# A twelve-stage decoder on one core: sums of x columns ahead of key rotations, waits of query turns split by bank, query copies ahead of exponentials in the first four steps

## The chip, the cores and the metric

The kernel runs on one core of a Trainium2 chip, all in one launch. The metric is the device time of that launch in microseconds (us). TensorE is called PE here, VectorE DVE, ScalarE ACT, GpSimd POOL, SyncE (which only issues DMAs) SP. Each engine runs its own list of instructions in the order in which it is written; engines wait for one another on semaphores that only count up.

## The reference

A decoder of four layers over x of 8 batches x 128 tokens x 512 columns, in float32. Every layer is a self-attention, a cross-attention to a context `ctx` of the same shape, and a feed-forward part, each followed by a norm of the sum with x: 12 stages. The stages that the change touches are the end of stage 0 (an attention inside each token) and stages 1 and 4, the cross-attentions of the first two layers, with 32 query heads and 8 key/value heads of 128 columns each. Per batch:

```python
queries = (q @ Wq.T).reshape(B, Sq, 32, 128).transpose(0, 2, 1, 3)      # from x
keys    = (k @ Wk.T).reshape(B, Skv, 8, 128).transpose(0, 2, 1, 3)      # from ctx
values  = (v @ Wv.T).reshape(B, Skv, 8, 128).transpose(0, 2, 1, 3)
queries, keys = _rope(queries), _rope(keys)          # x * cos + rotated(x) * sin
scores = einsum('bhqd,bhkd->bhqk', queries, repeat(keys, 4)) * 128 ** -0.5   # + mask
ctx = softmax(scores) @ repeat(values, 4)
return ctx.reshape(B, Sq, 32 * 128) @ Wd.T           # added to x, then the norm
```

## The kernel before

`build` writes, stage by stage, one list of instructions for each engine; `cross` is the function of stages 1 and 4. A cross stage has 8 groups g (one key/value head and its 4 query heads each) and in a group 8 batches b: 64 units u = 8g + b. xT, the transposed x of 1024 columns, comes from the stage before: its norm turns x batch by batch on PE (`norm.turn`, L174) and ACT copies the result to xT (`norm.copy`, L179).

**Queries.** The 512 x 512 by 512 x 1024 product of a group is not done as 8 block products but as 7, on sums of blocks (Strassen's way): P1 to P7, each of 2 chunks, each chunk 2 passes of 512 columns in the trace (x4 records for a product). DVE makes the sums of blocks of xT once a stage (`sums_of_xT`, L942 to L946, for batches 4 to 6 and then for batch 7), POOL those of the query weights once a group (`wq_sums`, L1062 to L1068) and those of the output weights (`wo_sums`, L1042 to L1048). The work of a group is cut into six jobs q0 to q5, called turns: q0 to q2 for the first two heads (p = 0), q3 to q5 for the other two. In a turn PE writes one bank with P1, P6, P7, which add up there, and its neighbour bank with the other product (P2, then P5 and P3, then P4). ACT copies the neighbour bank into QT (`QT<-banks`, L841, signal `x_other_here`); DVE then adds the first bank to it (L916, signal `x_qadd`). Turns 0 and 3 make block C11, turns 1 and 4 make C22's part and C12, turns 2 and 5 make C21 and C22.

- Turns 0, 3: P2, P1. Turns 1, 4: P5, P6, P3. Turns 2, 5: P4, P7.
- In `queries` (L667 to L717) PE waits ahead of a turn's first product until the last block of the turn before has been added (`x_qadd`), for both banks.

**Rotation.** For each of 2 key halves and 8 query blocks of a group DVE makes the sine part in `turned` (L898, L899; two buffers, so that a rotation waits for the last but one on POOL) and POOL the rest (L1073 and L1075; keys only L1075). The cosine part of keys is DVE's (L907).

**A step** of the main loop (step s, L775 on PE): scores of unit s (L787); the first job of the next group; transposes of the probabilities of unit s-2 (L797); the product with V (L815); the other jobs; from step 4 on the output product of earlier units, two units at a time by 7 products (`products`, L761), and from unit 48 on one by one (`plain`, L745). ACT in a step: exponentials (L865), copy of the first job, copy of the turned probabilities (L847), copy of the mixed values (L876), scaling of the probabilities (L882), copies of the other jobs. DVE in a step: scale and mask (L1011), maximum (L1013), addition of the first job (L916), inverse of the sums (L1025), the step's rotations for the next group (`turn_some`, whose numbers for group 1 are (1,1,2,1,1,1,1,0)), additions of the other jobs.

Which job stands in which step is the table `plans` (L552): for group 1's jobs, done in steps 0 to 7, (2,1,2,1,1,0,1,0): q0 and q1 in step 0, q2 in step 1, q3 and q4 in step 2, q5 in step 3, values in steps 4 and 6. The opening (L764 to L774) has both key products of group 0, the turn of batch 7, the six turns of group 0 in the order q0, q3, q1, q4, q2, q5, the values, and the key products of group 1.

## Time and profile before

| | us |
|---|---|
| median of 3 runs | 2729.45 |
| lowest, highest | 2726.92, 2735.56 |
| the profiled execution | 2729.9 |
| its span in the profile | 2728.6 |

The profile is of one execution. All its times are us from the start of the span unless marked ns. A row of the timeline is a run of like instructions: start, duration, engine, line, operation, out<-in tiles and shapes, count, and in brackets how long the engine was idle before it and whose end it waited for. A float32 matmul of one chunk is 2 records. The end of the last matmul of a run is modelled, so that a row is 0.16 us longer than the time until PE can start the next. The granted clock is the share of 2.4 GHz that TensorE got.

| part of the span | from, to |
|---|---|
| opening of stage 1 on PE | 165.96 to 216.76 |
| its steps 0 to 3 | 216.76 to 256.06 |
| its steps from 4 on, to step 52 | 256.06 to 750 |
| opening of stage 4 on PE | 1116.85 to 1168.39 |
| its steps 0 to 3 | 1168.39 to 1207.69 |

### The profile page before, as it was taken

How to read it: one execution, taken by the hardware profiler on the slowest of the kernel's cores; microseconds unless marked ns; L12 is line 12 of the kernel's file. 1: busy time of each engine (PE TensorE's matmuls, PEld its weight loads, DVE VectorE, ACT ScalarE, POOL GpSimd, SP SyncE). 2: the span in 40 equal slices, each digit the busy share in tenths (PEclk: the TensorE clock that was granted, in tenths of full speed). 3: DMA queues.
4: the chain of work that ended last, by engine and by line, in shares of the span. 5: the costliest groups of instructions: out<-in, count | busy, mean ns of one | idle time of the engine just before them, and what ended most of it. 6: DMA issues, size and time to landing. Idle time of an engine off the chain costs nothing.

```text
span 2728.6 us, 40847 instructions
## 1 busy us (share of the span) xinstructions
PE 2595.4 (95%) x15544; PEld 1716.9 (63%) x15544; DVE 1576.0 (58%) x2953; ACT 1068.3 (39%) x3270; POOL 710.0 (26%) x695
## 2 busy tenths in 40 slices
PE   8989999999998898899999999989998889999998
PEld 7855676766565666456676675647774455666664
DVE  3476666676546456666666665464556653344455
ACT  0014444444462455244444444614444312333330
POOL 1036334444212000363334442122120220000002
PEclk9989999999999899999999999999999999999999
DMA  8631101111001100111011110010000010000000
GB/s 183 88 122 52 33 11 39 39 40 39 16 1 39 47 2 2 47 39 39 4 39 39 39 39 16 1 71 31 2 1 28 21 64 28 15 27 1 12 1 31
DMA packets 53826, 94.91 MB, mean 35 GB/s; under 512 B 29408, under 2 KB 38560, under 8 KB 47488
## 3 DMA queue, kind: packets, MB, share of 16 engines
q1 hardware_dynamic: 53632, 92.30, 11.5%
q8 instruction: 125, 2.05, 0.3%
q14 instruction: 69, 0.57, 0.1%
HBM read 83.89 MB, written 8.39 MB: 34 GB/s over the span
## 4 chain that ended last, share of the span: by engine, by line
PE 87%; DVE 7%; ACT 3%; issue 1%; DMA 1%; POOL 0%; DVEq 0%; SPq 0%; POOLq 0%; ACTq 0%
PE banks L683 14%; PE banks L761 11%; PE banks L664 4%; PE banks L745 4%; PE banks L815 4%; PE banks L787 4%; PE banks L651 4%; PE banks L1922 3%; PE banks L303 3%; PE banks L1411 3%; PE banks L1974 3%; PE banks L2212 2%; PE banks L1951 2%; PE banks L2244 2%; PE banks L1927 2%; PE banks L2277 2%
## 5 line engine op out<-in xcount | busy, mean ns | idle before, releaser
L161 POOL TENSOR_TENSOR norm_spread<-norm_mv,const 128x1 f32<-128x1 f32 x96 | 20.8, 217 | 1173.0 <-DVE norm_mv L157 1173.0
L865 ACT ACTIVATE E_x<-S_x,sm_x 128x128 f32<-128x128 f32 x512 | 199.3, 390 | 283.6 <-DVE sm_x L1013 282.2
L1073 POOL TENSOR_TENSOR QT<-QT,const 128x512 f32<-128x512 f32 x128 | 170.2, 1330 | 503.4 <-DVE turned L899 503.4
L683 PE MATMUL banks<-xT,weights 128*128 128x512 f32 x512 | 238.9, 601 | 10.3 <-DVE QT L916 10.3
L977 DVE TENSOR_TENSOR x<-banks,x 128x256 f32<-128x256 f32 (+1 forms) x288 | 147.2, 511 | 125.4 <-PE banks L761 121.4
L761 PE MATMUL banks<-weights,OT 128*128 128x256 f32 x768 | 189.4, 379 | 0.0
L916 DVE TENSOR_TENSOR QT<-banks,QT 128x512 f32<-128x512 f32 x128 | 85.4, 688 | 160.6 <-ACT QT L841 148.5
L683 PEld LDWEIGHTS banks<-xT,weights 128*128 128x128 f32 x512 | 95.4, 192 | 121.2 <-issue 106.7
L1075 POOL TENSOR_TENSOR QT<-QT,turned 128x512 f32<-128x512 f32 x128 | 166.5, 1301 | 10.0
L876 ACT ACTIVATE OT<-banks 128x512 f32<-128x512 f32 x128 | 76.5, 597 | 229.3 <-PE banks L815 229.3
L761 PEld LDWEIGHTS banks<-weights,OT 128*128 128x128 f32 x768 | 141.8, 190 | 38.3 <-DVE x L977 11.7
L882 ACT ACTIVATE E_x<-E_x,sm_x 128x128 f32<-128x128 f32 x512 | 162.1, 390 | 5.3 <-DVE sm_x L1025 5.3
L2340 ACT ACTIVATE E_s<-banks,top_s 128x128 f32<-128x128 f32 x512 | 139.3, 383 | 62.1 <-DVE top_s L2437 62.1
L683 PE MATMUL banks<-weights 128*128 128x512 f32 x320 | 155.7, 602 | 2.2 <-DVE QT L916 2.1
L787 PEld LDWEIGHTS banks<-KT,QT 128*128 128x128 f32 x1024 | 133.9, 191 | 18.3 <-issue 13.4
L761 PE MATMUL banks<-weights 128*128 128x256 f32 x576 | 144.2, 386 | 0.0
L815 PE MATMUL banks<-PT,V 128*128 128x512 f32 x256 | 131.1, 593 | 4.3 <-ACT PT L847 4.3
L787 PE MATMUL banks<-KT,QT 128*128 128x128 f32 x1024 | 134.9, 275 | 0.0
L761 PEld LDWEIGHTS banks<-weights 128*128 128x128 f32 x576 | 102.6, 190 | 43.4 <-DVE x L977 27.6
L841 ACT ACTIVATE QT<-banks 128x512 f32<-128x512 f32 x128 | 75.2, 588 | 125.3 <-PE banks L683 124.9
L2333 ACT ACTIVATE PT_s<-banks 128x512 f32<-128x512 f32 x128 | 69.8, 596 | 137.3 <-PE banks L2277 137.3
L899 DVE TENSOR_TENSOR turned<-QT,const 64x512 f32<-64x512 f32 x128 | 120.8, 944 | 1.8
(311 smaller groups left out, 5219.8 us busy)
## 6 DMA issues: line engine op xcount, KB each, us to landing
weights<-in_L_xwq SPq DMA_DIRECT2D x16, 1024.0 KB, 4.9
weights<-in_L_xwo SPq DMA_DIRECT2D x16, 1024.0 KB, 4.9
weights<-in_L_xwk SPq DMA_DIRECT2D x16, 256.0 KB, 5.1
weights<-in_L_xwv SPq DMA_DIRECT2D x16, 256.0 KB, 2.6
weights<-in_L_ffn_W_base SPq DMA_DIRECT2D x3, 1024.0 KB, 4.8
weights<-in_L_xwq SPq DMA_DIRECT2D x4, 768.0 KB, 5.0
weights<-in_L_xwo SPq DMA_DIRECT2D x4, 768.0 KB, 5.7
xT<-in_xT SPq DMA_DIRECT2D x4, 512.0 KB, 9.6
```

The source lines that it names most:

```text
L651: mm = PE.matmul(psum[keys_bank(g, i)][:, :], views["wk"][:, k, :], ctxT[:, k, half_of(i)], start=k == 0, stop=k == KC - 1)
L683: mm = PE.matmul(to, left[:, k, head], moving, start=name in ("P1", "P2", "P4", "P5") and k == 0, stop=k == 1, skip_group_check=name in (" ...
L761: mm = PE.matmul(to, left[:, k, :], right[:, k, :], start=first and k == 0, stop=k == 1, skip_group_check=name in ("P6", "P7", "P3"))
L787: mm = PE.matmul(psum[2 + u % 2][:, rows_of(h)], QT[g % 2][:, h, rows_of(b)], KT[g % 2][:, rows_of(b)], start=True, stop=True)
L815: PE.matmul(psum[5][:, :], V[g % 2][:, b, :], PT[u % 2][:, :, :], start=True, stop=True).then_inc(*x_mix.one())
L865: ins = AC.activation(e[:, j, :], s[:, j, :], ACT.Exp, bias=sm[:, 0, j:j + 1], scale=1.0, accum_out=sm[:, 1, j:j + 1])
L882: ins = AC.activation(e[:, j, :], e[:, j, :], ACT.Copy, scale=sm[:, 2, j:j + 1])
L899: return DV.tensor_tensor(t[lo, :, :], four(source[hi, :]), spread(sin128[hi, :], 4), ALU.mult)
L977: DV.tensor_tensor(to, source, to, ALU.add).then_inc(*x_sum.one())
L1073: PO.tensor_tensor(four(to), four(to), spread(cos128, 4), ALU.mult).then_inc(*pool_step.one())
L1075: PO.tensor_tensor(four(to), four(to), turned[j % 2][:, :, :], ALU.add).then_inc(*x_roped.one())
L2340: ins = AC.activation(E[s % 2][:, 4 * half + j, :], scores_of(half)[:, j // 2, j % 2, :], ACT.Exp, bias=top[s % 2][:, 4 * half + j:4 * hal ...
```

## The change

1. **Opening, PE.** In stage 1 batch 6 of x is turned after the first key product of stage 1 and no longer at the end of stage 0; so the first key product stands ahead of it.
2. **Opening, DVE.** The sums of xT of batch 7 stand ahead of the key rotations. The two key rotations stand behind the additions of q0 and q3, and the first query rotation behind the second of them.
3. **Waits by bank.** In `queries` PE waits ahead of a turn's first product (neighbour bank) for ACT's copy of that bank alone, and for DVE's addition only ahead of the first product into the other bank. This holds for all groups.
4. **Steps 0 to 3.** The table of jobs becomes (1,1,2,2,1,0,1,0): q0, q1, q2 and q3, q4 and q5. On PE the second job stands ahead of the product with V. ACT copies the first job's blocks ahead of the exponentials, and scales ahead of the second job and of the copy of the mixed values. The numbers of `turn_some` stay.
5. **First plain product** (unit 48). PE waits for one addition less, that into columns 0 to 255 of x from the neighbour bank.

```diff
@@ heads: pe_heads
-                    for b in range(4, 7):
+                    for b in range(4, 6):
                         norm.turn(b)
@@ cross
-                plans = [(2, 1, 2, 1, 1, 0, 1, 0)] + [(2, 2, 1, 2, 1, 1, 1, 0)] * (G8 - 2)
+                plans = [(1, 1, 2, 2, 1, 0, 1, 0)] + [(2, 2, 1, 2, 1, 1, 1, 0)] * (G8 - 2)
+                def no_outs(step):
+                    return step < 4
@@ pe_cross: queries
-                        if turn:
-                            PE.wait_ge(*x_qadd(8 * g + place_of(g, p, ADDED[turn - 1][-1]) + 1))
-                        elif g and n:
-                            PE.wait_ge(*x_qadd(8 * g + 4))
                         if n == 1:
                             PE.wait_ge(*xwq_sums(g + 1))
                             if g == 0:
                                 PE.wait_ge(*xT_sums(2))
+                        if turn:
+                            PE.wait_ge(*x_other_here(8 * g + place_of(g, p, OTHER[turn - 1][-1], OTHER) + 1))
+                            sums_added = x_qadd(8 * g + place_of(g, p, ADDED[turn - 1][-1]) + 1)
+                        elif g and n:
+                            PE.wait_ge(*x_other_here(8 * g + 4))
+                            sums_added = x_qadd(8 * g + 4)
+                        else:
+                            sums_added = None
                         if turn == 0:
                             product("P2").then_inc(*x_other.one())
+                            if sums_added:
+                                PE.wait_ge(*sums_added)
                             product("P1").then_inc(*x_query.one())
                         elif turn == 1:
                             product("P5").then_inc(*x_other.one())
+                            PE.wait_ge(*sums_added)
                             product("P6")
...
                             product("P4").then_inc(*x_other.one())
+                            PE.wait_ge(*sums_added)
                             product("P7").then_inc(*x_query.one())
@@ pe_cross: plain
-                            PE.wait_ge(*x_sum(NA * pairs + u - 2 * pairs))
+                            PE.wait_ge(*x_sum(NA * pairs + u - 2 * pairs - (u == 2 * pairs)))
@@ pe_cross: opening and steps
-                    for kind, i in opening[:2]:
-                        job(0, kind, i)
+                    job(0, "k", 0)
+                    if stage == 1:
+                        before.turn(B - 2)
+                    job(0, "k", 1)
                     before.turn(B - 1)
...
                         plain(step, 0)
+                        if no_outs(step):
+                            for j in jobs_at(step, 1):
+                                job(*j)
...
                             PE.matmul(psum[5][:, :], V[g % 2][:, b, :], PT[u % 2][:, :, :], start=True, stop=True).then_inc(*x_mix.one())
-                        for j in jobs_at(step, 1):
-                            job(*j)
+                        if not no_outs(step):
+                            for j in jobs_at(step, 1):
+                                job(*j)
@@ act_cross (exps, mixed_copy, scale hold what stood in the loop before)
                     for step in range(units + 3):
+                        if no_outs(step):
+                            for j in jobs_at(step, 0):
+                                drain(*j)
+                            exps(step)
+                            if step >= 2:
+                                turned_copy(step - 2)
+                            scale(step)
+                            for j in jobs_at(step, 1):
+                                drain(*j)
+                            if step >= 2:
+                                mixed_copy(step - 2)
+                            continue
@@ dve_cross: opening
                     sums_of_xT(4, B - 1)
-                    for kind, i in opening[:2]:
-                        drain(0, kind, i)
                     sums_of_xT(B - 1, B)
                     done = 0
                     for n, (kind, i) in enumerate(opening[2:]):
                         drain(0, kind, i)
-                        while done < (1, 2, 3, 4, 5, 8)[n]:
+                        if n < 2:
+                            rope_keys(0, n)
+                        while done < (0, 2, 3, 4, 5, 8)[n]:
                             turn_queries(0, done)
                             done += 1
```

What stands in a row on PE at the end of stage 0 and the start of stage 1 (L336 is stage 0's last product, L174 the turns of x, L651 the key products, L683 the query products), before:

```order
L336 MATMUL banks<-const,o 64x64 x32
L174 MATMUL banks<-const,x 128x128 x12
L651 MATMUL banks<-ctxT,weights 128x512 x8
L174 MATMUL banks<-const,x 128x128 x4
L683 MATMUL banks<-xT,weights 128x512 x10
```

and now (L655 and L687 are the former L651 and L683):

```order
L336 MATMUL banks<-const,o 64x64 x32
L174 MATMUL banks<-const,x 128x128 x8
L655 MATMUL banks<-ctxT,weights 128x512 x4
L174 MATMUL banks<-const,x 128x128 x4
L655 MATMUL banks<-ctxT,weights 128x512 x4
L174 MATMUL banks<-const,x 128x128 x4
L687 MATMUL banks<-xT,weights 128x512 x10
```

The first key product, four records of the list, moved up over the turn of batch 6.

ACT from step 0 of stage 1 on (L865 exponentials, L841 a copy of a query block, L882 the scaling), before:

```order
L865 ACTIVATE E0_x1,sm0_x1<-S0_x1,sm0_x1 128x128 x4
L841 ACTIVATE QT1_1<-banks 128x512
L882 ACTIVATE E0_x1<-E0_x1,sm0_x1 128x128 x4
L841 ACTIVATE QT1_1<-banks 128x512 x2
L865 ACTIVATE E1_x1,sm1_x1<-S1_x1,sm1_x1 128x128 x4
L841 ACTIVATE QT1_1<-banks 128x512
L882 ACTIVATE E1_x1<-E1_x1,sm1_x1 128x128 x4
```

and now (L880, L861, L893 in their place):

```order
L861 ACTIVATE QT1_1<-banks 128x512
L880 ACTIVATE E0_x1,sm0_x1<-S0_x1,sm0_x1 128x128 x4
L893 ACTIVATE E0_x1<-E0_x1,sm0_x1 128x128 x4
L861 ACTIVATE QT1_1<-banks 128x512 x2
L880 ACTIVATE E1_x1,sm1_x1<-S1_x1,sm1_x1 128x128 x4
L893 ACTIVATE E1_x1<-E1_x1,sm1_x1 128x128 x4
L861 ACTIVATE QT1_1<-banks 128x512
```

The copies of the first job moved up over the exponentials, and with the new table the two copies of q1 stand in step 1.

DVE from step 2 of stage 1 on (L1011 mask, L1013 maximum, L916 an addition of a query block, L1025 inverse, L898 and L899 a rotation), before:

```order
L1011 SCALAR_TENSOR_TENSOR S0_x1<-banks,const 128x512
L1013 TENSOR_REDUCE sm2_x1<-S0_x1 128x4
L916 TENSOR_TENSOR QT1_1<-banks,QT1_1 128x512
L1025 RECIPROCAL sm2_x1<-sm2_x1 128x4
L898 TENSOR_TENSOR turned0_1<-QT1_1,const 64x512
L899 TENSOR_TENSOR turned0_1<-QT1_1,const 64x512
L898 TENSOR_TENSOR turned1_1<-QT1_1,const 64x512
L899 TENSOR_TENSOR turned1_1<-QT1_1,const 64x512
L916 TENSOR_TENSOR QT1_1<-banks,QT1_1 128x512
```

and now (L1050, L1052, L955, L1064, L937 and L938):

```order
L1050 SCALAR_TENSOR_TENSOR S0_x1<-banks,const 128x512
L1052 TENSOR_REDUCE sm2_x1<-S0_x1 128x4
L955 TENSOR_TENSOR QT1_1<-banks,QT1_1 128x512 x2
L1064 RECIPROCAL sm2_x1<-sm2_x1 128x4
L937 TENSOR_TENSOR turned0_1<-QT1_1,const 64x512
L938 TENSOR_TENSOR turned0_1<-QT1_1,const 64x512
L937 TENSOR_TENSOR turned1_1<-QT1_1,const 64x512
L938 TENSOR_TENSOR turned1_1<-QT1_1,const 64x512
L955 TENSOR_TENSOR QT1_1<-banks,QT1_1 128x512
```

The additions ahead of the two rotations are now the two of q2; the one behind them, which was q4's, is now q3's.

## Rows read from the trace of the kernel before

**Rows 1.** The page: busy time, chain by engine, two groups on GpSimd.

```profile
PE 2595.4 (95%) x15544; PEld 1716.9 (63%) x15544; DVE 1576.0 (58%) x2953; ACT 1068.3 (39%) x3270; POOL 710.0 (26%) x695
...
PE 87%; DVE 7%; ACT 3%; issue 1%; DMA 1%; POOL 0%; DVEq 0%; SPq 0%; POOLq 0%; ACTq 0%
...
L1073 POOL TENSOR_TENSOR QT<-QT,const 128x512 f32<-128x512 f32 x128 | 170.2, 1330 | 503.4 <-DVE turned L899 503.4
...
L1075 POOL TENSOR_TENSOR QT<-QT,turned 128x512 f32<-128x512 f32 x128 | 166.5, 1301 | 10.0
```

**Rows 2.** Timeline of PE, first cross opening (start, us, line, tiles, count, idle before).

```profile
163.99 1.97 PE L174 MATMUL banks<-const,x 128*128 128x128 f32 x8
168.17 0.66 PE L174 MATMUL banks<-const,x 128*128 128x128 f32 x4 [2.21 <-DVE x L167]
168.66 8.73 PE L651 MATMUL banks<-ctxT,weights 128*128 128x512 f32 x16
...
177.67 7.03 PE L683 MATMUL banks<-xT,weights 128*128 128x512 f32 x16
185.47 1.98 PE L683 MATMUL banks<-xT,weights 128*128 128x512 f32 x4 [0.77 <-DVE QT L916]
...
202.74 7.31 PE L664 MATMUL banks<-weights,ctxT 128*128 128x128 f32 x64
```

**Rows 3.** Windows: busy us by engine, granted clock (PEclk), DMA share, GB/s.

```profile
163.30:166.70 3.40, 2.66 (x22) 2.14 (x18) 2.14 (x5) 1.20 (x2) 0.00 (x0) 0.62 0.01 2
...
169.30:172.71 3.41, 3.41 (x5) 1.35 (x4) 3.41 (x3) 0.16 (x1) 3.24 (x3) 0.50 0.72 193
216.76:256.06 39.30, 33.49 (x101) 16.54 (x100) 23.12 (x32) 16.27 (x55) 23.61 (x18) 0.96 0.05 13
223.91:227.32 3.41, 3.41 (x5) 1.35 (x4) 1.41 (x2) 1.42 (x4) 2.00 (x3) 0.50 0.02 5
256.06:640.00 383.94, 383.90 (x1739) 265.95 (x1737) 259.59 (x452) 180.18 (x592) 158.70 (x120) 1.00 0.09 31
```

**Rows 4.** Timeline of DVE in the same opening.

```profile
169.96 1.61 DVE L942 TENSOR_TENSOR weights<-xT 128x384 f32<-128x384 f32 x1
...
177.40 0.68 DVE L898 TENSOR_TENSOR turned<-banks,const 64x512 f32<-64x512 f32 x1
...
181.74 1.38 DVE L944 TENSOR_TENSOR xT<-xT 128x128 f32<-128x128 f32 x1
...
184.74 0.68 DVE L916 TENSOR_TENSOR QT<-banks,QT 128x512 f32<-128x512 f32 x1
```

**Rows 5.** Timeline of PE, the waits of the first steps.

```profile
223.38 3.30 PE L683 MATMUL banks<-xT,weights 128*128 128x512 f32 x4 [2.14 <-DVE QT L916]
...
231.91 1.12 PE L683 MATMUL banks<-weights 128*128 128x512 f32 x2 [0.52 <-DVE QT L916]
...
242.58 1.13 PE L815 MATMUL banks<-PT,V 128*128 128x512 f32 x2 [1.45 <-ACT PT L847]
```

**Rows 6.** Timeline of ACT: a query copy behind the exponentials.

```profile
221.96 0.58 ACT L841 ACTIVATE QT<-banks 128x512 f32<-128x512 f32 x1
```

**Rows 7.** Timeline of DVE: half a rotation beside a busy GpSimd.

```profile
247.62 1.66 DVE L899 TENSOR_TENSOR turned<-QT,const 64x512 f32<-64x512 f32 x1
```

**Rows 8.** Timeline of POOL: sums of query weights, sums of output weights.

```profile
216.33 1.27 POOL L1062 TENSOR_TENSOR weights<-weights 128x512 f32<-128x512 f32 x1
...
241.10 1.27 POOL L1042 TENSOR_TENSOR weights<-weights 128x512 f32<-128x512 f32 x1
```

**Rows 9.** Timeline of PE, opening of the second cross stage.

```profile
1135.59 3.50 PE L683 MATMUL banks<-xT,weights 128*128 128x512 f32 x4 [4.30 <-DVE QT L916]
...
1154.38 7.31 PE L664 MATMUL banks<-weights,ctxT 128*128 128x128 f32 x64
```

**Rows 10.** Timeline of PE: the first plain product.

```profile
737.29 3.67 PE L745 MATMUL banks<-weights,OT 128*128 128x512 f32 x8 [0.97 <-DVE x L977]
```

**Rows 11.** Timeline of DVE: the last addition ahead of it.

```profile
736.73 0.41 DVE L977 TENSOR_TENSOR x<-banks,x 128x256 f32<-128x256 f32 x1
```

47 lines of the change are left out of this document (25 added, 22 removed).

## The prediction, worked out before the change ran

> **What bounds the kernel now.** I read the page first: PE is busy for 95% of the span and holds 87% of the chain that ended last [rows 1]. An edit therefore pays only where PE stands idle, or runs at the lower clock, inside the two cross stages. The windows say where that is: from 256.06 to 640.00 PE is busy for 383.90 of 383.94 us [rows 3]. The waits split by bank apply to every group, but in the groups of this stretch there is no wait to take away: worth 0 there. What is left are two openings, two times four first steps, and the first plain product.
>
> In the opening of stage 1 [rows 2] PE is idle for 2.21 us before the turn of batch 6. The key products behind it take 8.73 us, where the 16 like passes from 177.67 on take 7.03, because the granted clock was 0.50 from 169.30 to 172.71 [rows 3]. Then comes a wait of 0.77 us at 185.47, for DVE. In steps 0 to 3 PE is busy for 33.49 of 39.30 us [rows 3], so 5.81 are idle (the longest 2.14, 0.52 and 1.45 [rows 5]), and again the clock was 0.50, from 223.91 to 227.32 [rows 3]. 3.41 us at half clock are 1.7 us of work lost, of which 1.6 can be had back where PE waits a little anyway. Each restart also hides 0.16 us of modelled end. The work in these steps is 56 query passes (7.03/16 less the tail, 0.43 each, 24.0), 4 passes with V (1.7), 4 scores (3.6) and 2 transposes (0.9): 30.2. So 9.1 us a stage is all that the steps can give.
>
> **The openings.** *Stage 1, PE.* The last turn of stage 0 ends at 163.99 + 1.97 = 165.96 [rows 2]. Now the first key product (8 passes, 3.44) starts there, ends at 169.4, and the turn of batch 6 follows, whose norm was done at 168.1. The context and the weights are there: the DMA share from 163.30 to 166.70 is 0.01 [rows 3]. No idle 2.21 us, so I also expect no low clock behind it: second key product to 173.3, turn 7, q0 and q3 from 173.7 to 180.6 (before 177.67 to 184.54): **3.9 gained**. *DVE.* The sums of xT need batch 6's copy, now at 170.7 instead of 169.5, so they start 0.8 later than at 169.96 [rows 4], while POOL is busy less long beside them; they end at about 177.8 (before 177.40). The small sums took from 181.54 to 184.74, with one subtraction of 1.38 us beside POOL [rows 4]; they now follow at once, with POOL idle: 2.1 us, end 180.0. PE wants them at 180.6. The 0.77 + 0.16 is gone: **0.9**. *The price* is that the key rotations (2.1 each, 177.40 to 181.54 [rows 4]) and all that POOL does come later: the first query rotation reaches POOL at 187.7, not 186.9. POOL needs 1.33 + 1.30 = 2.63 us for a block [rows 1], DVE two halves of 0.7, or 1.66 beside POOL [rows 7]. Walking through the eight blocks with the two `turned` buffers I get POOL's last end at about 212.6, before 216.33 [rows 8]; PE reaches its scores at 216.76 - 4.9 = 211.9. The scores need six blocks, ready at 206.5. But the sums of the next query weights, 5.3 us from 216.33 on [rows 8], now end at 217.9, and PE wants them for q1 at 217.1: a new wait of 0.9 in step 0, the first place where the price is paid. *Stage 4* has the turn of batch 6 earlier already, so only DVE's part counts: the wait of 4.30 us before 1135.59, and the slow passes behind it (3.50 us for 4 records, 1.88 elsewhere) [rows 9]; PE would go on at 1131.3. q5 then ends at 1148.3 instead of 1154.38 [rows 9]: **6.1**. DVE is 0.8 us further ahead here, and the wait for the weight sums is about 0. Sum of the openings 3.9 + 0.9 + 6.1 = **10.9**.
>
> **Steps 0 to 3.** t counts from the start of scores 0. Step 0 of before: ACT copies q0's block at 221.96, behind the exponentials, although P2 was done at 219.4 [rows 6], DVE adds, and PE starts q1 at 223.38 [rows 5]. Now that copy is ahead, q1 moves into step 1 behind the scores, and the sum is added at t 5.3: the 2.14 and the low clock behind it go. In stage 1 q1 runs from 6.1 (weight sums) to 11.3. q2 follows scores 2 at 12.1: ACT's copy of C12 (12.0) and DVE's addition (12.75) are there for P4 and P7. DVE then does rotation 1, mask and maximum and both additions of q2 by 17.9; PE's P1 of q3 wants them at 17.8: wait 0.2. Then the expensive place. q3 is now a second job, so on DVE its addition stands behind `turn_some` of step 2, with two rotations, just when POOL is in the sums of the output weights (four operations from 241.10 on [rows 8], some 6 us). Half a rotation takes 1.66 us there [rows 7], so the two end 6.6 us after 18.45, q3's addition at 25.75, and PE, which has done P5 of q4 at 23.2, waits for P6: **2.6 us of new idle**. q5 then waits 0.4 for the copy of C12, which stands ahead of the exponentials. Scores 4 start at 34.5 in stage 1, 33.7 in stage 4, where before they started at 39.3: **4.8 and 5.6**. The move of the second job ahead of the product with V costs nothing: that product waits for ACT's copy of the turned probabilities (1.45 us, [rows 5]), which q3 now covers. From step 4 on DVE's mask comes 1.0 us behind the scores as before, and POOL is ahead of where it was.
>
> Which value for the 2.6? Its ends are 0, if DVE's halves take 0.7, and 3.5, if POOL's output sums and the next blocks hold both rotations throughout; I take 2.6, from the row that is the same operation at the same place. GPSIMD Engine Reference of the Trainium skill, section 1 (Specifications), says that GpSimd shares its SBUF interfaces with VectorE, in contention with instructions that have two SBUF inputs; by that rule a table which puts a rotation ahead of an addition under POOL's sums speaks against the change, and without it the forecast would be 5 us lower.
>
> **After an idle of 2.6 us** the clock may fall once more. It fell behind 2.21, 2.14 and 4.30 and not behind 0.77 or 1.45. A low stretch costs 1.6. I take it in one of the two stages: **-1.6**, ends 0 and -3.2.
>
> **The plain product.** PE waits 0.97 us at 737.29 [rows 10] for an addition that DVE ends at 737.14 [rows 11]. The remaining wait was met before, so each stage gains 0.97 + 0.16: **2.3**.
>
> **Sum.** 10.9 + 4.8 + 5.6 - 1.6 + 2.3 = 22.0. The profiled execution took 2729.9 (span 2728.6 and 1.3 around it), the median is 2729.45, which is 0.45 lower. 2729.9 - 22.0 = **2708**.
>
> **Rivals.**
> *The steps give nothing.* Each wait for an addition turns into one for POOL's weight sums, a copy or the exponentials behind the copy. Only the openings and the plain product stay: 13.2, 2717. For it: my walk already has four new waits in a stage. Against it: only one is long. 12%.
> *No wait is left in the steps.* 10.9 + 18.2 + 2.3 = 31.4 gained would be 2698.5; with some small waits 2701. It needs rotations at 0.7 us beside a busy POOL. 10%.
> *Low clock behind every short wait.* In the rows 0.52 and 0.77 left the clock high. TensorE: Matmul & The Clock Gate of the Trainium skill, on its second failure mode (psum-queue depth-cycling), says that frequent micro-idles between groups of matmuls make the clock oscillate. In this kernel that would be a low stretch behind each of my seven new waits: 23.6 - 7 x 1.6 = 12.4 gained, 2717.5. 5%.
> *The sums don't decide.* If in the opening PE, freed from the sums, waits as long for q0's addition at P6, about 5 us per stage come back: 2718. Against it: the addition is DVE's next operation behind the sums. 6%.
> *Slower.* The later key rotations push POOL's chain. Scores 0 need six query blocks, of which POOL starts the first at 187.7 and PE wants the last at 211.9: 4.0 us a block. If DVE's half pair beside POOL (3.3) and POOL's pair (2.6) came one after the other, a block would take 5.9, the scores would wait 11.4 a stage: 2708 + 22.8 + 1.6 = 2732. It decides from 4.0 us a block. Against it: two `turned` buffers let them overlap, and the mean of POOL's block is 2.63 [rows 1]. Even more than 5.9 is needed for slower by over 0.3%. 5%.
>
> **How the numbers follow.** Forecast 62%, the rivals 12, 10, 5, 6 and 5. The range takes the forecast's own bounds (2703 to 2713) and reaches to the rivals on both sides: 2701 to 2718, leaving out the slower case and the outer edges, under 2 in 10. About 0.3% (8 us, so 2721 and 2738) is what a measurement of this kernel can tell from no change. Faster 0.87 (all but the slower case and the upper edges of three rivals), same 0.10, slower 0.03.
>
> **What would show it.** Right: no idle ahead of the first key product and none at q1 in the openings; no granted clock of 0.50 between the first key product and scores 0; a PE wait of 2 to 3 us for a DVE addition in the middle of q4 of step 3; scores 4 of stage 1 some 9.7 us earlier than 256.06, those of stage 4 some 11.7 us earlier in their own stage; no wait ahead of the plain product. Wrong: PE waits at q1 of step 0 or 1 for POOL's weight sums by more than 2 us, or at scores 0 for a rotation, or any wait in steps 4 to 8 that was not there before.

## The result and the profile after

The changed kernel takes 2711.98 us (median of 4 runs, 2711.70 to 2717.03), the kernel before on the same chip 2730.48 (4 runs); the ratio is 0.9935 with a 95% interval of 0.9915 to 0.9955. The profiled execution took 2711.99 us, its span is 2710.7, 17.9 less than 2728.6. The forecast was 2708, 22.0 less.

The page of the changed kernel (busy time; chain that ended last) answers to [rows 1]:

```profile
PE 2587.2 (95%) x15544; PEld 1715.8 (63%) x15544; DVE 1582.3 (58%) x2953; ACT 1067.7 (39%) x3270; POOL 715.1 (26%) x695
...
PE 85%; DVE 8%; ACT 3%; issue 2%; POOL 1%; DMA 1%; DVEq 0%; SPq 0%; POOLq 0%; ACTq 0%
```

PE is still busy for 95% of a shorter span; GpSimd has come into the chain with 1%, and DVE has 8% of it. Where GpSimd stands in the chain shows in the timeline of PE in stage 1 (start, us, line, tiles, count, idle before and its releaser), against [rows 2, 5]:

```profile
165.28 3.70 PE L655 MATMUL banks<-ctxT,weights 128*128 128x512 f32 x8 [0.78 <-DVE x L422]
...
173.13 8.75 PE L687 MATMUL banks<-xT,weights 128*128 128x512 f32 x20
...
211.18 1.05 PE L803 MATMUL banks<-KT,QT 128*128 128x128 f32 x8
...
219.72 3.58 PE L687 MATMUL banks<-xT,weights 128*128 128x512 f32 x4 [3.16 <-POOL weights L1107]
...
240.81 1.98 PE L687 MATMUL banks<-weights 128*128 128x512 f32 x4 [2.13 <-DVE QT L955]
...
245.20 1.13 PE L687 MATMUL banks<-weights 128*128 128x512 f32 x2 [0.25 <-ACT QT L861]
...
249.59 1.05 PE L803 MATMUL banks<-KT,QT 128*128 128x128 f32 x8
```

The opening did what was foreseen. The first key product starts at 165.28 instead of behind the turn of batch 6. The idle of 0.78 ahead of it, for a DVE addition, was not foreseen, but it costs nothing here: the turns in front took 1.09 us, where before they took 1.97, partly at the lower clock, so the product starts 5.7 us behind the start of stage 0's last product, where the forecast had 5.8. And the 0.77 ahead of q1 in the opening is gone, since q0, q3 and the first of q1 are one row of 20 records; scores 0 start at 211.18. The wait of 2.14 us for q0's addition is gone too. In its place, at 219.72, PE waits 3.16 us for GpSimd's weight sums. The wait of P6 in q4 that was foreseen is there (2.13 at 240.81), and so is the small one for the copy of C12 (0.25).

Stage 4, against [rows 9]: no wait in the opening (it was 4.30 us), and the same two long ones in the steps.

```profile
1117.34 8.75 PE L687 MATMUL banks<-xT,weights 128*128 128x512 f32 x20
...
1163.48 1.98 PE L687 MATMUL banks<-xT,weights 128*128 128x512 f32 x4 [2.71 <-POOL weights L1107]
...
1182.80 1.98 PE L687 MATMUL banks<-weights 128*128 128x512 f32 x4 [1.96 <-DVE QT L955]
```

Windows of the changed kernel (busy us of PE, PEld, DVE, ACT, POOL; granted clock; DMA share; GB/s): steps 0 to 3 of stage 1, the low clock in them, 32 later steps of that stage, steps 0 to 3 of stage 4. They answer to [rows 3]:

```profile
211.18:249.59 38.41, 32.86 (x101) 16.39 (x100) 26.39 (x37) 17.25 (x59) 27.77 (x21) 0.96 0.03 7
219.55:222.97 3.42, 3.25 (x4) 1.51 (x5) 2.14 (x3) 1.33 (x5) 2.57 (x3) 0.50 0.00 0
359.00:680.27 321.27, 321.27 (x1442) 221.18 (x1441) 219.03 (x377) 149.11 (x489) 137.72 (x104) 1.00 0.10 34
1155.39:1191.59 36.20, 31.27 (x102) 15.74 (x101) 25.77 (x37) 17.24 (x59) 27.62 (x21) 1.00 0.03 7
```

The low clock of the opening and that of before from 223.91 on are gone; one stands behind the new 3.16 us wait, none behind the 2.71 of stage 4 or the two of 2.13 and 1.96.

And the first plain product, against [rows 10]:

```profile
728.78 3.60 PE L759 MATMUL banks<-weights,OT 128*128 128x512 f32 x8
```

It follows the products ahead of it with no idle.

The start of PE's rows gives the account by stretch. All are differences of the profiled executions, in us; "left as it is" is the part of the span that runs the same code in both.

| stretch | before | after | difference | forecast |
|---|---|---|---|---|
| stage 0's last product to scores 0 | 56.64 | 51.64 | -5.0 | -4.9 |
| steps 0 to 3, stage 1 | 39.30 | 38.41 | -0.9 | -4.8 |
| steps 4 to 47, stage 1 | 431.59 | 430.68 | -0.9 | 0 |
| steps 48 to 62, stage 1 | 126.89 | 125.68 | -1.2 | -1.1 |
| first key product to scores 0, stage 4 | 51.54 | 45.46 | -6.1 | -6.1 |
| steps 0 to 3, stage 4 | 39.30 | 36.20 | -3.1 | -5.6 |
| steps 4 to 47, stage 4 | 431.39 | 430.76 | -0.6 | 0 |
| steps 48 to 62, stage 4 | 126.93 | 125.71 | -1.2 | -1.1 |
| left as it is | 1425.0 | 1426.1 | +1.1 | 0 |
| low clock charged ahead of time | | | | +1.6 |
| sum | 2728.6 | 2710.7 | -17.9 | -22.0 |

Two things did not come as forecast. The first four steps gave 4.0 us instead of 10.4, or instead of 8.8 when the low clock that the forecast charged apart is counted with them (one such stretch is in the 38.41). And the later steps gave 1.5 us that nobody had forecast.

### The profile page after: what moved, and what is told of

Its sections match the earlier page's. It is cut to its first block, busy times and chain, and to the rows that moved or that the text cites. A ratio compares the mean times of both kernels' runs of the same rounds, so it can differ in the third digit from the quotient of the medians.

```text
span 2710.7 us, 40847 instructions
## 1 busy us (share of the span) xinstructions
PE 2587.2 (95%) x15544; PEld 1715.8 (63%) x15544; DVE 1582.3 (58%) x2953; ACT 1067.7 (39%) x3270; POOL 715.1 (26%) x695
## 4 chain that ended last, share of the span: by engine, by line
PE 85%; DVE 8%; ACT 3%; issue 2%; POOL 1%; DMA 1%; DVEq 0%; SPq 0%; POOLq 0%; ACTq 0%
PE banks L687 13%; PE banks L775 11%; PE banks L759 4%; PE banks L834 4%; PE banks L803 4%; PE banks L668 4%; PE banks L655 3%; PE banks L1961 3%; PE banks L1450 3%; PE banks L303 3%; PE banks L2013 3%; PE banks L2251 2%; PE banks L2283 2%; PE banks L1990 2%; PE banks L1966 2%; PE banks L2316 2%
## 5 line engine op out<-in xcount | busy, mean ns | idle before, releaser
L880 ACT ACTIVATE E_x<-S_x,sm_x 128x128 f32<-128x128 f32 x512 | 199.2, 390 | 262.0 <-DVE sm_x L1052 260.5
L687 PE MATMUL banks<-xT,weights 128*128 128x512 f32 x512 | 236.7, 596 | 5.9 <-POOL weights L1107 5.9
L687 PEld LDWEIGHTS banks<-xT,weights 128*128 128x128 f32 x512 | 95.0, 191 | 113.6 <-issue 105.8
L775 PEld LDWEIGHTS banks<-weights,OT 128*128 128x128 f32 x768 | 141.8, 190 | 38.3 <-DVE x L1016 11.7
L893 ACT ACTIVATE E_x<-E_x,sm_x 128x128 f32<-128x128 f32 x512 | 162.1, 390 | 1.0 <-DVE sm_x L1064 1.0
L955 DVE TENSOR_TENSOR QT<-banks,QT 128x512 f32<-128x512 f32 x128 | 85.3, 687 | 129.6 <-ACT QT L861 127.7
L687 PE MATMUL banks<-weights 128*128 128x512 f32 x320 | 153.2, 594 | 4.6 <-DVE QT L955 4.1
L803 PEld LDWEIGHTS banks<-KT,QT 128*128 128x128 f32 x1024 | 133.9, 191 | 18.3 <-issue 13.2
L861 ACT ACTIVATE QT<-banks 128x512 f32<-128x512 f32 x128 | 75.3, 588 | 142.7 <-PE banks L687 142.3
L938 DVE TENSOR_TENSOR turned<-QT,const 64x512 f32<-64x512 f32 x128 | 130.4, 1018 | 1.8
```

The lines of the kernel that those rows point to most:

```text
L687: mm = PE.matmul(to, left[:, k, head], moving, start=name in ("P1", "P2", "P4", "P5") and k == 0, stop=k == 1, skip_group_check=name in (" ...
L775: mm = PE.matmul(to, left[:, k, :], right[:, k, :], start=first and k == 0, stop=k == 1, skip_group_check=name in ("P6", "P7", "P3"))
L803: mm = PE.matmul(psum[2 + u % 2][:, rows_of(h)], QT[g % 2][:, h, rows_of(b)], KT[g % 2][:, rows_of(b)], start=True, stop=True)
L880: ins = AC.activation(e[:, j, :], s[:, j, :], ACT.Exp, bias=sm[:, 0, j:j + 1], scale=1.0, accum_out=sm[:, 1, j:j + 1])
L893: ins = AC.activation(e[:, j, :], e[:, j, :], ACT.Copy, scale=sm[:, 2, j:j + 1])
L938: return DV.tensor_tensor(t[lo, :, :], four(source[hi, :]), spread(sin128[hi, :], 4), ALU.mult)
```

## Experiments

**The question.** The openings gave 11.1 us, the steps behind them 6.4 too little (4.8, if the low clock that the forecast charged apart is counted with them). *Theory:* the edit of DVE's opening puts the key rotations later, the chain of rotations on DVE and GpSimd does not become shorter with PE's way, and GpSimd's sums of the next query weights, which stand behind that chain, become the last thing that q1 waits for. Then the openings' gain is partly given back. *Rival:* the new order of the steps gives little by itself, whatever the opening. First each part alone, and the wait itself.

### The steps without the opening edits

```diff
@@ the changed kernel
-                    for b in range(4, 6):
+                    for b in range(4, 7):
                         norm.turn(b)
-                    job(0, "k", 0)
-                    if stage == 1:
-                        before.turn(B - 2)
-                    job(0, "k", 1)
+                    for kind, i in opening[:2]:
+                        job(0, kind, i)
...
                     sums_of_xT(4, B - 1)
+                    for kind, i in opening[:2]:
+                        drain(0, kind, i)
                     sums_of_xT(B - 1, B)
...
-                            PE.wait_ge(*x_sum(NA * pairs + u - 2 * pairs - (u == 2 * pairs)))
+                            PE.wait_ge(*x_sum(NA * pairs + u - 2 * pairs))
```

> The changed kernel with both opening edits and the plain product as in the kernel before: the new table of jobs, ACT's and PE's new order in steps 0 to 3 and the waits by bank stay. Theory (price of the later key rotations): GpSimd is not pushed back here, its sums of the next query weights end some 4.9 us behind the start of scores 0 as before, and q1 wants them at 5.2, so PE has no wait on GpSimd in step 0 or 1. Steps 0 to 3 then take 33 to 34 us in each cross stage (39.3 before, 38.4 and 36.2 after), and the kernel some 11 to 13 us less than before, about 2718. Rival (the new order of the steps itself gives little): 36 us or more per stage with a wait of 2 us or more of another name, and at most 7 us gained.

The windows of its steps 0 to 3 in stages 1 and 4:

```profile
215.11:248.50 33.39, 31.00 (x101) 15.69 (x100) 23.89 (x33) 17.24 (x59) 24.85 (x19) 1.00 0.03 9
1165.20:1198.43 33.23, 31.00 (x101) 15.67 (x100) 23.75 (x33) 17.24 (x59) 24.70 (x19) 1.00 0.03 8
```

33.4 and 33.2 us, at full clock throughout: 5.9 and 6.1 less than before. The only wait of more than 0.3 us in each is the one of q4, here stage 1's:

```profile
239.72 1.99 PE L687 MATMUL banks<-weights 128*128 128x512 f32 x4 [2.14 <-DVE QT L953]
```

So the new steps, which here include the waits by bank, are worth 6 us a stage, as long as GpSimd is not late. The rival falls. (The waits by bank alone, two sections on, take 3.4 of these 5.9 us in stage 1; the new order by itself was not run.) The kernel as a whole took 2723.81 us (ratio 0.9968, 0.9955 to 0.9982), less of a gain than the 11 to 13 expected: its cross stages are 13.2 us shorter, but the code that is the same in all kernels took 6.3 us more in its profiled execution (see the last section).

### The opening edits alone

```diff
@@ the kernel before
-                    for b in range(4, 7):
+                    for b in range(4, 6):
                         norm.turn(b)
-                    for kind, i in opening[:2]:
-                        job(0, kind, i)
+                    job(0, "k", 0)
+                    if stage == 1:
+                        before.turn(B - 2)
+                    job(0, "k", 1)
...
                     sums_of_xT(4, B - 1)
-                    for kind, i in opening[:2]:
-                        drain(0, kind, i)
                     sums_of_xT(B - 1, B)
                     done = 0
                     for n, (kind, i) in enumerate(opening[2:]):
                         drain(0, kind, i)
-                        while done < (1, 2, 3, 4, 5, 8)[n]:
+                        if n < 2:
+                            rope_keys(0, n)
+                        while done < (0, 2, 3, 4, 5, 8)[n]:
```

> The kernel before with the two opening edits alone. Both theories: openings 5.0 and 6.1 us shorter. Theory: GpSimd's weight sums then end about 8.5 us behind the start of scores 0, and q1, which before waited until 6.6 for its addition, now waits until 8.5 for them: steps 0 to 3 take about 41 us instead of 39.3, and the kernel gains 7 to 8 us (about 2722). Rival: the steps stay at 39.3 and the gain is 11 us.

Windows of its steps 0 to 3, PE's row at q1, and GpSimd's last weight sum:

```profile
212.61:254.13 41.52, 33.49 (x101) 16.58 (x100) 25.32 (x35) 16.25 (x55) 26.23 (x20) 0.96 0.06 13
1164.64:1206.14 41.50, 33.49 (x102) 16.52 (x100) 25.15 (x35) 16.25 (x55) 26.05 (x20) 0.96 0.05 13
```

```profile
221.46 3.68 PE L683 MATMUL banks<-xT,weights 128*128 128x512 f32 x4 [4.36 <-DVE QT L918]
```

```profile
218.93 1.26 POOL L1070 TENSOR_TENSOR weights<-weights 128x512 f32<-128x512 f32 x1
```

The openings are 4.2 and 5.7 us shorter. The steps take 41.5 us in both stages, 2.2 more than before, close to the 41 of the theory. But the last thing q1 waited for was not the weight sums, ready at 220.2; it was q0's addition at 221.4. Both hang on the same chain: DVE can rotate the second key half of group 1 only when GpSimd has given the `turned` buffer of the last block back, and mask, maximum, exponentials, copy and addition come behind that. The stretch with the same code as before cost 9.6 us more here, and the kernel took 2732.59 us (ratio 1.0000, 0.9989 to 1.0011): instead of the 7 to 8 us that were expected, this edit on its own could not be told from no change, though PE's way through the cross stages had become 5.5 us shorter in the profile.

### The waits by bank alone

```diff
@@ the kernel before
                     def queries(g, n):
-                        if turn:
-                            PE.wait_ge(*x_qadd(8 * g + place_of(g, p, ADDED[turn - 1][-1]) + 1))
-                        elif g and n:
-                            PE.wait_ge(*x_qadd(8 * g + 4))
+                        if turn:
+                            PE.wait_ge(*x_other_here(8 * g + place_of(g, p, OTHER[turn - 1][-1], OTHER) + 1))
+                            sums_added = x_qadd(8 * g + place_of(g, p, ADDED[turn - 1][-1]) + 1)
+                        elif g and n:
+                            PE.wait_ge(*x_other_here(8 * g + 4))
+                            sums_added = x_qadd(8 * g + 4)
...
```

> The kernel before with the waits by bank alone. In the steps of all later groups PE had no idle to give. In steps 0 to 3 P5 of q1 can start before q0's addition, but ACT's copy stands behind the exponentials and the addition follows it by 0.1 us, so the 2.14 us wait shrinks by 0.8 at most, and the other waits of 0.5 go: 1 to 2.5 us per stage. In the openings the wait for the x sums is the last one and stays. 2 to 5 us in all, about 2726. If more than 8 us are gained, the waits by bank are the change's main part.

```profile
216.12:252.05 35.93, 31.09 (x102) 15.87 (x101) 22.61 (x32) 16.20 (x55) 23.61 (x18) 1.00 0.06 15
361.35:682.63 321.28, 321.28 (x1442) 221.32 (x1441) 218.99 (x377) 149.01 (x489) 137.71 (x104) 1.00 0.10 34
1167.52:1205.07 37.55, 32.72 (x102) 16.50 (x101) 22.46 (x32) 16.24 (x55) 23.45 (x18) 0.95 0.06 13
```

Steps 0 to 3 take 35.9 us in stage 1 (-3.4) and 37.6 in stage 4 (-1.8, with a low clock in it that costs 1.7). That is more than I expected; the wait at q1 shrank from 2.14 to 1.43 and took its low clock along. The middle row is the surprise: steps 16 to 47 take 321.28 us, where the kernel before took 322.36. PE counts as busy for 322.32 of the one and all of the other, at the same clock, so what went are idles too short to be shown as waits, 0.27 us a group. The changed kernel has the same 321.27. Against this, steps 4 to 7 take 0.4 us longer, with a new wait of 0.35 for an addition to x. In all its cross stages are 6.5 us shorter, and the kernel took 2727.49 us (ratio 0.9988, 0.9977 to 0.9999), 2.2 less than the kernel before, where 2 to 5 were expected.

### The wait for the weight sums cut in three

```diff
@@ the changed kernel, queries
                         if n == 1:
-                            PE.wait_ge(*xwq_sums(g + 1))
+                            PE.wait_ge(*xwq_first(g + 1))
...
                             product("P5").then_inc(*x_other.one())
                             PE.wait_ge(*sums_added)
+                            if n == 1:
+                                PE.wait_ge(*xwq_third(g + 1))
                             product("P6")
+                            if n == 1:
+                                PE.wait_ge(*xwq_sums(g + 1))
@@ wq_sums
-                        PO.tensor_tensor(a21, a21, a22, ALU.add).then_inc(*pool_step.one())
-                        PO.wait_ge(*pool_step.all())
-                        PO.tensor_tensor(QS[:, 0], a21, a11, ALU.subtract).then_inc(*pool_step.one())
-                        PO.wait_ge(*pool_step.all())
+                        PO.tensor_tensor(a21, a21, a22, ALU.add).then_inc(*xwq_first.one())
+                        PO.wait_ge(*xwq_first(g + 1))
+                        PO.tensor_tensor(QS[:, 0], a21, a11, ALU.subtract).then_inc(*xwq_third.one())
+                        PO.wait_ge(*xwq_third(g + 1))
```

> The changed kernel with PE's wait for the weight sums cut into three: P5 waits for the second of GpSimd's four operations, P6 for the third, P3 for the fourth. Theory: P5 of q1 starts 2.7 us earlier, where GpSimd's second operation ends; the waits of 3.16 and 2.71 us shrink to about 0.6 and 0.1 and the low clock behind the first goes: 5 to 7 us less than the changed kernel, about 2705.5. Rival (something else is as late, such as the addition of q0 or the copy): under 2 us gained.

```profile
217.60 1.99 PE L688 MATMUL banks<-xT,weights 128*128 128x512 f32 x4 [0.46 <-POOL weights L1108]
...
222.31 1.96 PE L688 MATMUL banks<-xT,weights 128*128 128x512 f32 x4 [1.02 <-ACT QT L866]
...
238.97 1.98 PE L688 MATMUL banks<-weights 128*128 128x512 f32 x4 [2.13 <-DVE QT L960]
```

The 3.16 us wait became 0.46, and no low clock followed. But 1.02 us came back three products later, for ACT's copy of C22: on ACT that copy stands behind exponentials and scaling, and P5 now ends before they do. Steps 0 to 3 take 36.0 us in stage 1 (38.4) and 37.1 in stage 4, where this time a low clock stands behind the wait of q4 (35.4 without it). The kernel took 2709.34 us (ratio 0.9925, 0.9910 to 0.9940): the expected 5 to 7 us were about 3 in the steps, since a part of the wait was owed to the next in line.

### GpSimd's cosine products of the opening left out

```diff
@@ the changed kernel, pool_cross
-                            rope(NR * g + 2 + m, query(g, *rotated(g)[m]), True)
+                            rope(NR * g + 2 + m, query(g, *rotated(g)[m]), g > 0)
```

> The changed kernel with GpSimd's cosine product of the eight query blocks of group 0 left out (so the rotation of these blocks is incomplete): 8 operations of 1.3 us less on GpSimd in each opening, nothing changed on PE, ACT and DVE. Theory (the chain of rotations on GpSimd and DVE in the opening, 3.6 us a block, makes the weight sums late): the chain ends 5 us or more earlier, the waits of 3.16 and 2.71 us at q1 and the low clock go, and steps 0 to 3 take 33.2 to 33.6 us in both stages, as without the opening edits; about 2704. Rival (the weights' load or DVE's own list, not GpSimd, is late): a wait of over 1 us at q1 stays.

```profile
210.75:245.83 35.08, 32.70 (x101) 16.27 (x100) 22.90 (x33) 17.25 (x59) 20.54 (x16) 0.95 0.03 8
235.93:239.35 3.42, 3.42 (x6) 1.36 (x5) 0.69 (x1) 0.00 (x0) 3.34 (x3) 0.50 0.00 0
1150.39:1183.62 33.23, 31.01 (x102) 15.67 (x100) 22.75 (x33) 17.25 (x59) 20.38 (x16) 1.00 0.02 8
```

With GpSimd's chain some 8 operations shorter and PE's, ACT's and DVE's lists untouched, both waits at q1 are gone; the waits left in the steps are 2.13 (1.97) and 0.25. Stage 4's steps take 33.2 us, stage 1's 35.1 with a low clock from 235.93 on, 33.4 without. These are the times of the kernel without opening edits. So it is the chain of rotations with GpSimd in it, not the load of the weights nor DVE's list by itself, that takes 5.0 and 3.0 us of the openings' 11.1 back. The edit does not part GpSimd's own time from what it does to DVE: with the products gone, four of DVE's eight second halves in the opening of stage 1 fell from 1.66 to 0.69 us too. The two runs took 2704.00 and 2708.71 us.

### DVE's opening undone in the changed kernel

```diff
@@ the changed kernel
                     sums_of_xT(4, B - 1)
+                    for kind, i in opening[:2]:
+                        drain(0, kind, i)
                     sums_of_xT(B - 1, B)
                     done = 0
                     for n, (kind, i) in enumerate(opening[2:]):
                         drain(0, kind, i)
-                        if n < 2:
-                            rope_keys(0, n)
-                        while done < (0, 2, 3, 4, 5, 8)[n]:
+                        while done < (1, 2, 3, 4, 5, 8)[n]:
```

> The changed kernel with DVE's opening as before: key rotations ahead of the sums of batch 7 and of the query blocks. Theory: the wait for the x sums comes back (3.7 to 4.2 us in stage 1, 3.7 in stage 4, each with a low clock), but GpSimd has started its rotations earlier against PE, so the waits for the weight sums go: openings 4 and 6 us longer, steps 5 and 3 us shorter than in the changed kernel. Net +2 to +4 us, about 2715. Rival (DVE's new opening brings its full 7 to 10 us): 2719 or more.

PE's row at q1 of the opening, and the windows of steps 0 to 3 ("issue" says that the profile shows no releaser; DVE's last sum of x ends at 184.17, 0.1 us ahead of the row):

```profile
184.27 3.09 PE L687 MATMUL banks<-xT,weights 128*128 128x512 f32 x4 [4.18 <-issue]
```

```profile
217.22:252.30 35.08, 32.70 (x101) 16.25 (x100) 23.88 (x33) 17.25 (x59) 24.85 (x19) 0.95 0.03 8
1159.81:1194.74 34.93, 32.70 (x102) 16.26 (x101) 23.75 (x33) 17.25 (x59) 24.70 (x19) 0.95 0.03 8
```

The exchange is as the theory has it: a wait of 4.18 us for the x sums comes back in the opening (3.75 in stage 4), the wait for the weight sums goes, and the steps take 35.1 and 34.9 us, each with a low clock that costs 1.7; without it 33.4 and 33.2. The size is between the two expectations: openings 6.1 and 5.7 us longer, steps 3.3 and 1.3 shorter, cross stages 7.3 us longer than in the changed kernel, 5.6 if the low clocks in the steps of both are left out. The kernel took 2717.73 us (ratio 0.9952, 0.9937 to 0.9967). So DVE's new opening is worth 6 to 7 of the 11.8 us that its own stretches show.

Set side by side, the profiles of stage 1 also say what in the opening makes the sums late. All times count from the start of stage 0's last product:

| | first query rotation on GpSimd | weight sums ready | scores 0 | sums behind scores 0 |
|---|---|---|---|---|
| the kernel before | 26.8 | 61.5 | 56.6 | 4.9 |
| the changed kernel | 27.3 | 60.1 | 51.6 | 8.5 |
| DVE's opening undone | 26.8 | 62.7 | 57.8 | 4.9 |
| without cosine products | 27.3 | 52.0 | 51.7 | 0.3 |

The chain starts within 0.5 us of the same place in all four. The later key rotations hardly move it; the sums are even ready 1.4 us earlier than before. They are late only against PE, which is at scores 0 5.0 us earlier.

### A rotation out of step 2

The other wait, 2.1 us ahead of P6 of q4, is the one that the prediction had from DVE's row of rotations.

```diff
@@ the changed kernel
-                shares = [(1, 1, 2, 1, 1, 1, 1, 0)] + [(0, 1, 1, 2, 1, 1, 1, 1)] * (G8 - 2)
+                shares = [(1, 1, 1, 1, 2, 1, 1, 0)] + [(0, 1, 1, 2, 1, 1, 1, 1)] * (G8 - 2)
```

> The changed kernel with one of the two rotations of step 2 moved to step 4 (numbers 1,1,1,1,2,1,1,0). Theory (q3's addition is late because two rotations of 1.66 us halves stand ahead of it on DVE): the waits of 2.13 and 1.96 us ahead of P6 of q4 go, 4 us less in all, about 2708; steps 4 to 8 stay at 29.1 us. Rival (the rotations are wanted where they were): steps 4 to 8 take 1 us or more longer.

```profile
259.29 1.13 PE L775 MATMUL banks<-weights 128*128 128x256 f32 x4 [1.41 <-DVE x L1016]
...
269.33 1.13 PE L775 MATMUL banks<-weights,OT 128*128 128x256 f32 x4 [0.56 <-DVE weights L999]
```

The wait went in both stages (steps 0 to 3: 36.0 and 33.9 us, 2.4 and 2.3 less). But steps 4 to 7 take 30.9 us instead of 29.1: the rotation now stands ahead of an addition to x, for which PE waits 1.41, and ahead of the sums of mixed values (0.56). 1.8 of 2.3 us were handed to the next step; the rival was right on this half. 2710.05 us (0.9922, 0.9905 to 0.9938).

Both small edits together:

> Both small edits together: PE's wait for the weight sums cut in three, and a rotation moved from step 2 to step 4. Theory: they add up, 36.0 us of the steps in stage 1 become 33.8 and 35.4 (at full clock) in stage 4 become 33.3: 2.5 us from the one and 4 us from the other, about 2705.

They add up in the steps: 33.5 and 33.1 us, at full clock, behind them 30.9 as with the rotation alone. 2706.97 us (0.9914, 0.9896 to 0.9932).

### Where the rotation may go

Two more places for that rotation, with the wait cut in three, and the changed kernel again on the same chip:

```diff
-                shares = [(1, 1, 1, 1, 2, 1, 1, 0)] + [(0, 1, 1, 2, 1, 1, 1, 1)] * (G8 - 2)
+                shares = [(1, 1, 1, 1, 1, 2, 1, 0)] + [(0, 1, 1, 2, 1, 1, 1, 1)] * (G8 - 2)
@@ or
+                shares = [(1, 1, 1, 1, 1, 1, 1, 1)] + [(0, 1, 1, 2, 1, 1, 1, 1)] * (G8 - 2)
```

> As the kernel with the wait cut in three and one rotation moved, but the rotation is moved to step 5 (numbers 1,1,1,1,1,2,1,0), where DVE has no sums of mixed values ahead of it and no query block to add. Theory (in step 4 the second rotation stood ahead of an addition to x, PE waited 1.4 and 0.6 us there): steps 4 to 8 fall from 30.9 to 29.1 to 29.5 us, steps 0 to 3 stay at 33.1 to 33.5; 3 us less over both stages. Rival (any second rotation in steps 4 to 7 costs the same): 30.5 us or more.

```profile
266.21 1.10 PE L780 MATMUL banks<-weights,OT 128*128 128x256 f32 x4 [1.17 <-DVE x L1021]
269.21 2.07 PE L780 MATMUL banks<-weights,OT 128*128 128x256 f32 x4 [1.90 <-DVE weights L1004]
```

Step 5 is the worst of the places tried: waits of 1.17 and 1.90 us, in stage 1 a low clock with the second, and 33.2 and 31.9 us for steps 4 to 7. The rival was right. My reason was true and not enough: the sums of mixed values stand in steps 4 and 6, not in 5, but step 5 has additions to x, and the sums of step 6 come close behind its rotations. DVE's list shows it:

```profile
265.63 0.42 DVE L1021 TENSOR_TENSOR x<-banks,x 128x256 f32<-128x256 f32 x1
...
267.29 0.41 DVE L1001 TENSOR_TENSOR weights<-banks,OT 128x256 f32<-128x256 f32 x1
```

The rotations end at 265.61 and the addition for which PE waits stands right behind them; the sums of mixed values follow from 267.29. The kernel took 2718.55 us (0.9951, 0.9938 to 0.9964).

> The same with the last rotation of group 1 in step 7 (numbers 1,1,1,1,1,1,1,1), so that no step has two. Theory: steps 4 to 8 at 29.0 to 29.3 us, steps 8 to 16 at 80.3 as long as GpSimd has the last block by step 12. Within 1 us of the kernel with two rotations in step 5.

Windows of steps 0 to 3 and 4 to 7, stage 1 and stage 4:

```profile
211.62:245.22 33.60, 31.56 (x101) 15.77 (x100) 22.97 (x35) 17.26 (x59) 24.51 (x19) 1.00 0.03 9
245.22:273.84 28.62, 28.62 (x178) 24.30 (x176) 21.05 (x40) 16.25 (x56) 14.73 (x12) 1.00 0.14 47
1150.72:1183.91 33.19, 31.57 (x102) 15.77 (x101) 22.56 (x35) 17.25 (x59) 24.38 (x19) 1.00 0.03 8
1183.91:1212.52 28.61, 28.61 (x178) 24.27 (x177) 21.04 (x40) 16.25 (x56) 14.70 (x12) 1.00 0.15 47
```

One rotation in each step leaves PE busy for all of steps 4 to 7 (28.62 of 28.62 us) and 33.6 and 33.2 us for steps 0 to 3. Its two cross stages take 1275.8 us, 8.7 less than those of the changed kernel (1284.5), and its time is below that of the kernel before and of the changed kernel: 2708.02 us (0.9913, 0.9900 to 0.9927), where the changed kernel on the same chip had 2716.72. Against the kernel with the second rotation in step 4 (0.9914, on another chip) its cross stages are 4.4 us shorter, but the total does not show it.

> The changed kernel once more, on the same chip as the two above, for a direct comparison. Its stretches as in its first profile to 0.2 us, but for the low clock, whose place differs from run to run; 4 to 8 us above the two others.

2716.72 us (6 runs, 2709.71 to 2720.78; ratio 0.9945, 0.9930 to 0.9960): 8.7 above the kernel with a rotation in step 7, but 1.8 below the one with two in step 5, where 4 to 8 above had been expected. Its openings and steps 16 to 62 repeat to 0.1 us; its steps 0 to 3 took 40.2 and 37.9 us, with 3.4 us more of low clock in each than in the first profile. The kernel with the rotation in step 7 is not within 1 us of the one with it in step 5, as expected, but 8 us better in the cross stages.

## Why the prediction was right, and where it was not

**What bounds the kernel: right.** Idle PE time inside the cross stages is what was won. The sign and the range (2701 to 2718) held; the forecast was 4 us too low. In part that is luck: 1.5 us from later steps that the prediction put at nothing stand against 4.8 missing in the first ones, and code that no edit touches moves the total by more than this miss (last section).

**Its own signs.** Of the signs of being wrong one came in full, PE's wait at q1 for the weight sums of more than 2 us, in both stages. Another came in small: a wait in step 5 that was not there before, 0.45 us in stage 1 and 0.38 in stage 4. No wait for a rotation came at scores 0. Scores 4 came 5.9 us earlier in stage 1 and 9.2 in stage 4, counted from the start of the opening's stretch, for 9.7 and 11.7.

```profile
260.95 1.13 PE L775 MATMUL banks<-weights 128*128 128x256 f32 x4 [0.45 <-DVE x L1016]
```

**Openings: right to 0.1 us.** 5.0 and 6.1 gained for 4.9 and 6.1. The key product ran where the turn had waited, the low clock behind it went, the x sums were ready before q1.

**Steps 0 to 3: the mechanisms right, one size wrong.** The failing step is "Walking through the eight blocks with the two `turned` buffers I get POOL's last end at about 212.6", and with it "a new wait of 0.9 in step 0" and, for stage 4, "about 0". They were 3.16 and 2.71. The price as such was also misread: the first query rotation reached GpSimd at 186.83, not at 187.7, so nothing was paid for a later start; what was short is the time for the eight blocks, 24.9 us in the walk and 27.6 in the profile. GpSimd's and DVE's rows show the fault:

```profile
186.83 1.76 POOL L1112 TENSOR_TENSOR QT<-QT,const 128x512 f32<-128x512 f32 x1 [0.63 <-DVE turned L938]
188.67 1.61 POOL L1114 TENSOR_TENSOR QT<-QT,turned 128x512 f32<-128x512 f32 x1
190.24 1.27 POOL L1112 TENSOR_TENSOR QT<-QT,const 128x512 f32<-128x512 f32 x1
...
211.78 1.27 POOL L1112 TENSOR_TENSOR QT<-QT,const 128x512 f32<-128x512 f32 x1 [0.63 <-DVE turned L938]
...
218.41 1.27 POOL L1107 TENSOR_TENSOR weights<-weights 128x512 f32<-128x512 f32 x1
```

```profile
210.04 1.66 DVE L938 TENSOR_TENSOR turned<-QT,const 64x512 f32<-64x512 f32 x1
...
215.91 0.69 DVE L946 TENSOR_TENSOR KT<-banks,const 128x512 f32<-128x512 f32 x1
...
236.72 1.64 DVE L937 TENSOR_TENSOR turned<-QT,const 64x512 f32<-64x512 f32 x1
```

The first block starts at 186.83, the eighth at 211.78: 3.56 us a block, where the walk comes to about 3.2. I had walked with 2.6 for GpSimd's pair and allowed DVE's halves to be slowed; but while DVE's half takes 1.66 for 0.69, GpSimd's operations take 1.6 to 1.8 for 1.27, and GpSimd then waits 0.63 more for DVE's second half. Each slows the other, so the chain ends at 214.40, and the weight sums at 219.68, 8.5 us behind scores 0 (4.9 before), where q1 wants them at 5.2. Section 1 of GPSIMD Engine Reference of the Trainium skill speaks of contention between the two engines; I had applied it to DVE alone. The trace agrees, and in both directions.

There was a sign of it in the kernel before. There the weight sums were ready 4.9 us behind scores 0:

```profile
220.37 1.27 POOL L1068 TENSOR_TENSOR weights<-weights 128x512 f32<-128x512 f32 x1
```

In its own list q1 could not start before 6.6, for q0's addition. In the new list that wait is gone and q1 wants the sums at 5.2. A chain with 0.3 us of room cannot let 5 us of PE's idle go for nothing. I had that slack in hand and still took the price of the later rotations from a walk that was too kind.

**The wait of q4: right.** 2.6 forecast, 2.13 and 1.96 measured, at the product and from the operation that were named.

**Low clock: right in the sum, wrong in the place.** One low stretch in the two stages, but behind the 3.16 us wait that I had at 0.9. That it was one is luck: the same kernel profiled again had three in these steps.

**Plain product: right.** 1.2 a stage for 1.1.

**Waits by bank in later groups: wrong.** "Worth 0 there" was 0.27 us a group in stage 1 and 0.2 to 0.27 in stage 4, 1.5 us in all with the small new wait of steps 4 to 7 taken off. PE's busy time in the windows counts the modelled end of a matmul, and so covered idles of a fraction of a microsecond.

**The rivals.** "The steps give nothing" at 12% was the closest of them to what happened, since 40% of their gain came; its mechanism, a wait that turns into one for the weight sums, was the right one. "Slower" named the right chain and too high a point: scores 0 would have been late from 4.0 us a block on, but the weight sums, further back on the same queue, are late from about 3.0 us a block: q1 wants them at 211.18 + 5.2, they take 5.3, and the eight blocks start at 186.83 (worked out from the rows, not run). In the cross stages of the changed kernel the clock did not fall behind the waits of 0.25 to 0.45 us, nor with the weight sums waited for in parts behind one of 1.02, as the rival from the second failure mode of TensorE: Matmul & The Clock Gate of the Trainium skill would have had it. It is not ruled out elsewhere: ahead of stage 4 the changed kernel has a low stretch from 1103.61 on beside waits of 0.38, 0.81 and 1.50 us that follow one another within 4.1 us.

## What to carry to other kernels

Before you price an edit that lets one engine arrive earlier, list what else it wants at that place and how much room each has: with 0.3 us of room on GpSimd's sums, a gain of 5.0 us in the opening of stage 1 went again in a wait for them and the low clock behind it, and 3.0 of 6.1 us in stage 4. Two engines that slow each other must be walked with the slow time for both. And read such a change by stretch, from scores to scores: at full clock the stretches repeat to 0.1 or 0.2 us, while the total moves by more than the edit is worth; a low clock inside a stretch has to be taken off first.
